# Second attention's output bank: three heads at rows 0, 34 and 68 in place of two at rows 0 and 64

## What is computed

```python
x = L0_attn_x                                   # (2, 512, 512)
x = _layernorm(x + _L0_attn_ref(x, ...))        # 32 heads of 128, sliding window
x = _layernorm(x + _L0_ffn_ref(x, ...))         # gated, 1376 wide
x = _layernorm(x + _L1_attn_ref(x, ...))        # 32 heads of 16, 8 key/value groups, causal
x = _layernorm(x + _L1_ffn_ref(x, ...))         # 512x512 and a low-rank part by 8 experts

# the attention of the second layer
scores = jnp.einsum('bhqd,bhkd->bhqk', q, k_h) / math.sqrt(HEAD_DIM)
scores = jnp.where(causal[None, None], jnp.finfo(scores.dtype).min, scores)
attn = jax.nn.softmax(scores, axis=-1)
ctx = jnp.einsum('bhqk,bhkd->bhqd', attn, v_h)
```

## Time and profile before

| | |
|---|---|
| median of 3 runs | 1215.43 us |
| profiled execution | 1214.89 us |
| its span, first to last instruction | 1213.3 us |
| granted TensorE clock, mean | 0.997 |
| TensorE matmul busy | 1180.8 us (97%), 6698 instructions |
| TensorE weight load busy | 1023.2 us (84%) |
| VectorE busy | 799.6 us (66%) |
| ScalarE busy | 752.5 us (62%) |
| GpSimd busy | 548.3 us (45%) |

### The profile page before, as it was taken

The page is one execution under the profiler, slowest core; times in us unless marked ns, Lnnn a source line. Parts: engine busy times, 40 slices in busy tenths (PEclk is TensorE's granted clock), DMA queues, the critical chain, the costliest instruction groups (busy, mean ns, idle before and its releaser), DMA issues. The chain is left out here.

```text
span 1213.3 us, 21135 instructions
## 1 busy us (share of the span) xinstructions
PE 1180.8 (97%) x6698; PEld 1023.2 (84%) x6698; DVE 799.6 (66%) x2575; ACT 752.5 (62%) x1758; POOL 548.3 (45%) x519
## 2 busy tenths in 40 slices
PE   7899999999999999999999999999999999999997
PEld 6788888888888888888888788888887999999886
DVE  6757776667766677766777722223458888888685
ACT  6656765566655567655665454441129999999624
POOL 4554454444533554534533233331136766676400
PEclk9999999999999999999999999999999999999999
DMA  6011110011110111101000022220002213220001
GB/s 223 18 44 36 35 36 28 22 43 27 46 34 12 44 36 35 36 27 35 27 1 27 18 70 78 61 97 1 18 20 53 65 41 108 48 48 21 1 1 70
DMA packets 30368, 51.28 MB, mean 42 GB/s; under 512 B 5680, under 2 KB 6576, under 8 KB 30256
## 3 DMA queue, kind: packets, MB, share of 16 engines
q1 hardware_dynamic: 29680, 48.85, 13.7%
q10 hardware_dynamic: 576, 1.05, 0.2%
HBM read 38.35 MB, written 2.10 MB: 33 GB/s over the span
## 5 line engine op out<-in xcount | busy, mean ns | idle before, releaser
L487 POOL TENSOR_TENSOR turned<-turned,sin 128x512 f32<-128x512 f32 x73 | 94.4, 1293 | 311.5 <-ACT turned L347 311.5
L363 ACT ACTIVATE probs<-probs,neg_max 128x256 f32<-128x256 f32 (+1 forms) x256 | 119.8, 473 | 14.0 <-DVE neg_max L580 14.0
L1484 ACT ACTIVATE a_probs<-a_probs,a_neg_max 128x512 f32<-128x512 f32 (+3 forms) x256 | 123.2, 571 | 0.1
L1720 DVE CUSTOM_DVE_ANT_0 a_probs<-bank,a_mask 128x512 f32<-128x512 f32 (+3 forms) x256 | 109.7, 485 | 0.2 <-PE bank L1949 0.2
L490 POOL TENSOR_TENSOR turned<-turned,by_cos 128x512 f32<-128x512 f32 x73 | 101.1, 1385 | 5.7
L96 PE MATMUL bank<-wo_hi,oT_hi 128*128 128x512 f32 x256 | 100.3, 392 | 1.7 <-DVE oT_lo L643 1.7
L734 PE MATMUL bank<-xT_hi,wq_hi 128*128 128x512 f32 x256 | 101.7, 397 | 0.0
L734 PE MATMUL bank<-xT_lo,wq_hi 128*128 128x512 f32 x256 | 100.2, 391 | 0.0
L734 PE MATMUL bank<-xT_hi,wq_lo 128*128 128x512 f32 x256 | 100.1, 391 | 0.0
L96 PE MATMUL bank<-wo_hi,oT_lo 128*128 128x512 f32 x256 | 99.9, 390 | 0.0
L96 PE MATMUL bank<-wo_lo,oT_hi 128*128 128x512 f32 x256 | 99.7, 389 | 0.0
(11 more groups left out here) (239 smaller groups left out, 3454.0 us busy)
## 6 DMA issues: line engine op xcount, KB each, us to landing
staged<-weights SPq DMA_DIRECT2D x70, 256.0 KB, 2.7
f_staged<-weights_f SPq DMA_DIRECT2D x33, 256.0 KB, 2.7
a_q_stack<-a_qT_hi SPq DMA_DIRECT2D x64, 64.0 KB, 2.0
rows<-x_rows SPq DMA_DIRECT2D x2, 1024.0 KB, 7.4
a_k_stack<-a_kT_hi SPq DMA_DIRECT2D x64, 32.0 KB, 2.0
a_q_stack<-a_qT_lo SPq DMA_DIRECT2D x32, 64.0 KB, 2.0
out<-rows SPq DMA_DIRECT2D x8, 256.0 KB, 2.0
a_raw<-weights_qkv SPq DMA_DIRECT2D x4, 384.0 KB, 4.9
```

Source lines behind the costliest of these rows:

```text
L363: act.activation(probs[:, s % 2, h, 0:width], probs[:, s % 2, h, 0:width], ACT.Exp, bias=neg_max[:, s % 2, h:h + 1], scale=SCALE0, accum_o ...
L487: pool.tensor_tensor(at, at, sin[:, :], ALU.mult).then_inc(sin_done, 1)
L1484: act.activation(row_probs(s, qt), row_probs(s, qt), ACT.Exp, bias=neg_max[:, h, qt:qt + 1], scale=-1.0).then_inc(exp_done, 1)
L1720: dve.tensor_tensor_reduce(row_probs(s, qt), ps_s[bank][:, at:at + seen], mask[:, SEQ - seen:SEQ], -SCALE1, HIGHEST, ALU.add, ALU.min, neg ...
```

## The change

The heads are grouped in packs of three (`PACK`), each head on 34 rows (`PACK_COLS`), at rows 0, 34 and 68, so that 102 rows (`OUT_ROWS`) are in use. A batch has 32 heads, so each batch begins with a pack of two and goes on with ten of three: 22 packs. A pack may run across two units. `PACK_OF` gives a head's pack and its place, `PACK_AT` the slot in which a pack is copied, turned, joined and finished: two slots after its last head's own slot, as before. The copy of the bank moves from ScalarE to VectorE, where it stands ahead of the maxima of its slot. `v_now` is 170 columns wide in place of 192, and the window is 102 columns in place of 128. The transposes move 102 columns and not 128.

```diff
+PACK_COLS = 2 * HD1 + 2
+PACK = 3
+OUT_ROWS = PACK * PACK_COLS
+V_AT = OUT_ROWS - PACK_COLS
+PACKS = []
+for _first in range(0, SLOTS1, SLOTS1 // BATCH):
+    _at, _end = _first, _first + SLOTS1 // BATCH
+    while _at < _end:
+        _size = PACK if (_end - _at) % PACK == 0 else 2
+        PACKS.append((_at, _size))
+        _at += _size
+PACK_OF = {_at + _n: (_i, _n) for _i, (_at, _size) in enumerate(PACKS) for _n in range(_size)}
+PACK_AT = {_at + _size + 1: _i for _i, (_at, _size) in enumerate(PACKS)}
...
-            def evacuate(n):
-                act.wait_ge(applied, 2 * (n + 1))
-                if n >= 1:
-                    act.wait_ge(o_turned, n)
-                act.activation(oT_now[:, :], ps_o[:, :], ACT.Copy).then_inc(o_read, 1)
...
-                if s % 2 == 1 and s >= 3:
-                    evacuate((s - 3) // 2)
...
-                if s % 2 == 1 and s >= 3:
-                    finish((s - 3) // 2)
+                if s in PACK_AT:
+                    finish(PACK_AT[s])
...
+            def evacuate(n):
+                dve.wait_ge(applied, PACKS[n][0] + PACKS[n][1])
+                if n >= 1:
+                    dve.wait_ge(o_turned, n)
+                dve.tensor_copy(oT_now[0:OUT_ROWS, :], ps_o[0:OUT_ROWS, :]).then_inc(o_read, 1)
+
             def join(n):
-                turned = ps_turn[:, :].rearrange("p (t h d) -> p t h d", t=SEQ_TILES, h=2)
+                size = PACKS[n][1]
+                turned = ps_turn[:, :].rearrange("p (t c) -> p t c", t=SEQ_TILES)[:, :, 0:size * PACK_COLS].rearrange(
+                    "p t (h d) -> p t h d", d=PACK_COLS)
...
             for s in range(SLOTS1 + 2):
+                if s in PACK_AT:
+                    evacuate(PACK_AT[s])
                 if s + AHEAD_MAXIMA < SLOTS1:
                     maxima(s + AHEAD_MAXIMA)
...
-                if s % 2 == 1 and 3 <= s < SLOTS1 + 1:
-                    join((s - 3) // 2)
+                if s in PACK_AT and s < SLOTS1 + 1:
+                    join(PACK_AT[s])
...
-                if h % 2 == 0 and s >= 2:
-                    pe.wait_ge(o_read, s // 2)
+                pack, place = PACK_OF[s]
+                if place == 0 and pack >= 1:
+                    pe.wait_ge(o_read, pack)
...
-                window = HALF - (h % 2) * HALF
+                window = V_AT - place * PACK_COLS
...
-                        mm = pe.matmul(ps_o[:, kb * P:SEQ], v_now[:, u % 2, kb, window:window + P],
+                        mm = pe.matmul(ps_o[0:OUT_ROWS, kb * P:SEQ], v_now[:, u % 2, kb, window:window + OUT_ROWS],
...
-                    mm = pe.transpose(ps_turn[:, j * P:(j + 1) * P], oT_now[:, j * P:(j + 1) * P], ident[:, :])
+                    mm = pe.transpose(ps_turn[:, j * P:j * P + OUT_ROWS], oT_now[0:OUT_ROWS, j * P:(j + 1) * P],
+                                      ident[0:OUT_ROWS, 0:OUT_ROWS])
...
-                if s % 2 == 1 and s >= 3:
-                    turn_output((s - 3) // 2)
+                if s in PACK_AT:
+                    turn_output(PACK_AT[s])
```

More of the change, by code:

```diff
@@ L1294, in attention1 @@
         oT_now = sb("oT_now", [P, SEQ])
-        o_sum = sb("o_sum", [P, SEQ_TILES, 2, HD1])
+        o_sum = sb("o_sum", [P, SEQ_TILES, PACK, HD1])
         by_at = aligned(nc.sbuf_base)
@@ L1298, in attention1 @@
         neg_max = sb("neg_max", [P, GROUP1, SEQ_TILES])
-        inv_sum = sb("inv_sum", [P, SEQ_TILES, 2])
+        inv_sum = sb("inv_sum", [P, SEQ_TILES, PACK])
         outT_hi, outT_lo = qT_hi, qT_lo
@@ L1614, in _ @@
             pool.wait_ge(pads_set, 2)
-            pool.memset(v_now[:, :, :, HALF + ONE_AT:HALF + ONE_AT + 1].bitcast(F32), 1.0).then_inc(pads_set, 1)
+            pool.memset(v_now[:, :, :, V_AT + ONE_AT:V_AT + ONE_AT + 1].bitcast(F32), 1.0).then_inc(pads_set, 1)
             def turn_rows(tile):
@@ L1636, in finish @@
             def finish(n):
-                u, pair = divmod(n, 2)
-                b, g = divmod(u, KV1)
-                at = g * GROUP_COLS + pair * PAIR_ROWS
+                first, size = PACKS[n]
+                b, head = divmod(first, HEADS1)
                 pool.wait_ge(summed, n + 1)
[L1641 to L1644, removed]
+                pool.tensor_tensor(o_tok[:, b * SEQ_TILES:(b + 1) * SEQ_TILES, head * HD1:(head + size) * HD1].rearrange(
+                    "p t (h d) -> p t h d", d=HD1), o_sum[:, :, 0:size, :],
+                                   inv_sum[:, :, 0:size].rearrange("p t (h a) -> p t h a", a=1).broadcast_to(
+                                       [P, SEQ_TILES, size, HD1]), ALU.mult).then_inc(finished, 1)
             def raise_diagonal(k):
@@ L1735, in join @@
                     dve.wait_ge(finished, n)
-                dve.reciprocal(inv_sum[:, :, :], turned[:, :, :, ONE_AT]).then_inc(inv_done, 1)
-                dve.tensor_copy(o_sum[:, :, :, :], turned[:, :, :, HD1:2 * HD1]).then_inc(low_read, 1)
+                dve.reciprocal(inv_sum[:, :, 0:size], turned[:, :, :, ONE_AT]).then_inc(inv_done, 1)
+                dve.tensor_copy(o_sum[:, :, 0:size, :], turned[:, :, :, HD1:2 * HD1]).then_inc(low_read, 1)
                 dve.wait_ge(low_read, n + 1)
                 dve.wait_ge(inv_done, n + 1)
-                dve.tensor_tensor(o_sum[:, :, :, :], turned[:, :, :, 0:HD1], o_sum[:, :, :, :], ALU.add).then_inc(summed, 1)
+                dve.tensor_tensor(o_sum[:, :, 0:size, :], turned[:, :, :, 0:HD1], o_sum[:, :, 0:size, :],
+                                  ALU.add).then_inc(summed, 1)
             for tile in range(TILES - 1):
@@ L1834, in _ @@
             low_out(0)
-            join(PAIRS1 - 1)
+            join(len(PACKS) - 1)
             for tile in range(1, 4):
@@ L1967, in apply @@
                     for part in (pT_hi, pT_lo):
-                        mm = pe.matmul(ps_o[:, kb * P:SEQ], v_now[:, u % 2, kb, window:window + P],
+                        mm = pe.matmul(ps_o[0:OUT_ROWS, kb * P:SEQ], v_now[:, u % 2, kb, window:window + OUT_ROWS],
                                        part[:, s % 2, piece, at:at + width],
-                                       start=(h % 2 == 0 and kb == 0 and part is pT_hi),
-                                       stop=(h % 2 == 1 and kb == KEY_TILES[-1] and part is pT_lo),
+                                       start=(place == 0 and kb == 0 and part is pT_hi),
+                                       stop=(place == PACKS[pack][1] - 1 and kb == KEY_TILES[-1] and part is pT_lo),
                                        skip_group_check=True)
@@ L2073, in _ @@
             turn_out(1)
-            turn_output(PAIRS1 - 1)
+            turn_output(len(PACKS) - 1)
             turn_out(2)
```

10 lines of the change are left out of this document (4 added, 6 removed).

## The result

| | before | changed |
|---|---|---|
| median | 1215.38 us (1215.1 to 1216.92, 4 runs) | 1201.42 us (1200.92 to 1203.3, 4 runs) |
| profiled execution, span | 1214.89, 1213.3 | 1201.25, 1199.6 |
| granted TensorE clock, mean | 0.997 | 0.996 |

What follows compares the result with a forecast made beforehand. ScalarE bound the second attention's loop, through its output copy L1501; TensorE would be next. 48 x (3.344 - 3.16) = 8.8, plus 0.4 and 0.5, less 1.2, gains 8.5 us: 1206.9, range 1202.9 to 1213.0.

Steps and rivals of the forecast that it cites:

- TensorE's terms: Second attention's loop: a slot costs TensorE 3.00 us, one with a turned output 3.48, so 9.48 for three slots.
- The copy's price: The copy of the bank from PSUM on VectorE, 102x512, estimated at 0.64 us, bounds 0.5 and 0.7.
- VectorE's pace: Rival, chance 0.20: VectorE with the added copy bounds the loop at 3.25 us a slot, gain 4.5, time 1211.
- The slow weight loads: Rival, chance 0.02: apply's loads of 102 columns go at half the pace, 0.22 us each, 11 us more, 1226.
- the 29.9 us: VectorE's wait for ScalarE ahead of L1728, read as idle time over the stage that makes the added copy fit.
- the hand-over loss: Ordinary slots: three engines within 4% of each other hand over less than ideally; 0.025 us x 48 = 1.2 taken off.
- the price of narrower operands: Apply's stationary and the transposes at 102 columns: taken as zero, bounds 0.06 us an apply either way, 0.1 a pack less.
- the gain of the last eight heavy slots: Slots 10 to 13 and 44 to 47, with weight halves on GpSimd: 0.4 us, only from calmer neighbours.
- my 3.22: Slots with a weight half: GpSimd bounds them at 3.02 us plus a share of finish, no difference by the change.
- The end of the loop: Last copy of the bank: 0.60 us on ScalarE becomes 0.64 on VectorE, which has nothing else ready; taken as zero.
- more than 12.5 us of gain: Rival, chance 0.03: narrower loads and transposes both shorten, ScalarE's 3.06 us a slot bounds, gain 14, at best 1201.
- The range's low end: Whole kernel, 1202.9 us: handing over free and both widths paying in part.

## Why the prediction was right in kind and too small

The gain by stretch, from the starts of TensorE's weight loads (turn of slot 0, then applies), with the forecast split in the same way:

| stretch | before | changed | gain | forecast | gain with 124 columns |
|---|---|---|---|---|---|
| turn 0 to apply 5 | 25.08 | 24.10 | 0.98 | 0.5 | 1.00 |
| 5 to 10 | 16.32 | 15.54 | 0.78 | 0.8 | 0.44 |
| 10 to 14 | 13.75 | 12.60 | 1.15 | 0.2 | 1.17 |
| 14 to 44 | 100.32 | 93.07 | 7.25 | 4.8 | 5.47 |
| 44 to 48 | 14.10 | 13.41 | 0.69 | 0.2 | 0.82 |
| 48 to 61 | 43.42 | 39.67 | 3.75 | 2.1 | 3.14 |
| 61 to 63 | 4.94 | 5.68 | -0.74 | 0 | -0.74 |
| sum | | | 13.9 | 8.5 | 11.3 |

The column with 124 columns is the run with copy and transposes of 124 rows too.

**What held.** Taking L1501 off ScalarE frees the loop, and TensorE becomes the bound: the pairs with VectorE's copy and the runs with wider operands show it. TensorE's terms held too, 3.00 a slot and 0.48 a turned output: the pairs take 6.46 for 6.48, the stage with 124 columns 94.85 for 95.3. The copy's price was 0.68 for 0.64. It lands beside the split and ahead of TensorE, with 0.46 of room where 0.35 was worked out. VectorE's pace was the nearest rival, and one more copy a pack made it true. The slow weight loads did not come: a load takes 168 ns, less than the 189 of before. One reading was off without harm: the 29.9 us that VectorE waited for ScalarE are those of the whole loop, not of the thirty slots, where that wait is 12.8 us.

In short, the step that failed is the sum. It named the right bound, but three of its terms were mis-sized: the hand-over loss (1.2 taken off, none there), the price of narrower operands (0 taken, 2.6 measured) and the gain of the last eight heavy slots (0.4 taken, 1.84 measured).

The difference, 5.4 us, is 2.6 from the widths (13.9 against 11.3 in the table) and 2.8 that were there with 124 columns too: 1.4 in the ordinary slots (9.05 against 7.7), 1.6 in the eight heavy ones (1.99 against 0.4), 0.5 in the first, less 0.74 at the end. By the same rates the four columns from 124 to 128 are some 0.5 more of the widths (an estimate, 2.5 x 4 / 22), within the 2.8.

**The hand-over term failed, 1.2 us.** I took 0.025 a slot off because a pair of before takes 6.69 where ScalarE's own work is 6.63. That loss belonged to ScalarE as the bound: it stands in one order behind results of the others. TensorE as the bound loses nothing that shows: with all its operands at 128 columns a pair takes 6.46 us, and the bare sum is 3.00 + 3.48. A loss at hand-overs isn't carried from one bounding engine to another without a row for it. Two smaller terms were missing from the ordinary slots and nearly cancel: they hold 17 turned outputs (2, 11 and 4 in the three stretches) and not 16, 0.5 us more, and slot 61, the last step of the stretch from apply 48, has no scores to make, so that its turn and the next stand 2.34 apart and not 2.96 (1108.58 and 1110.92), 0.6 us less. The missing scores are most of why the stretch behind slot 48 gained 1.0 more than forecast with 124 columns too; in the kernel before the same thirteen slots took 43.42, their full 13 x 3.344.

**The two widths failed, 2.6 us.** Stationary and transposes were taken as zero, with bounds of 0.06 an apply and 0.1 a pack. Measured are 0.04 an apply and 0.04 a pack for 22 columns. These were inside the bounds but only on one side: nothing in the trace spoke for a narrower operand that takes longer, while the earlier trace rows show ten loads one behind another at 0.11 us each, which shorter loads could only improve. Zero was the end of a one-sided range, not its middle.

**The heavy slots failed, 1.6 us.** I held that GpSimd is the bound there, at 3.02 + 0.2, and gave the last eight 0.4 us. In part it is: in the kernel before its casts of slots 45 to 48 follow one another without a gap, 3.43, 3.36 and 3.43 apart, from those of the earlier trace rows on:

```profile
1077.54 0.60 POOL L1631 CAST a_xT<-a_pT_raw 128x512 fp32r<-128x512 f32 x1
...
1080.97 0.61 POOL L1631 CAST a_xT<-a_pT_raw 128x512 fp32r<-128x512 f32 x1
```

But these are above my 3.22, the windows show 13.75 and 14.10 for four slots, and the first of these casts waited 0.74 for an apply. In the pairs with VectorE's copy GpSimd does the same work, and the eight slots take 12.93 and 13.33: the copy's place gives 0.8 us in each window. So these slots were held up by ScalarE's chain too, and the change reached them. The packs add 0.33 in slots 10 to 13 and nothing in 44 to 47 (13.41). The eight slots gained 1.84 us. That a late split held up ScalarE's copy, and with it the exponentials, is shown by the copy on ScalarE alone (4.42 us); in the kernel before only 0.2 us of such a wait is printed in each window. GpSimd's timeline of the changed kernel in slots 45 to 48:

```profile
1060.49 0.62 POOL L1636 CAST a_xT<-a_pT_raw 128x512 fp32r<-128x512 f32 x1
...
1063.58 0.61 POOL L1636 CAST a_xT<-a_pT_raw 128x512 fp32r<-128x512 f32 x1
...
1066.92 0.60 POOL L1636 CAST a_xT<-a_pT_raw 128x512 fp32r<-128x512 f32 x1
...
1070.47 0.61 POOL L1636 CAST a_xT<-a_pT_raw 128x512 fp32r<-128x512 f32 x1
```

3.09, 3.34 and 3.55 from cast to cast, without gaps: GpSimd is still the bound there, where a half meets a value split or a `finish`. A half without either goes through at the pace. This fits that spreading the work pays 1.9 us in this kernel; why it pays only 0.7 in the one before was not tested.

**Not in the sum.** Slots 0 to 4 gave 0.5 more than forecast; the cause is open. The end of the loop lost 0.74, and I had looked there only at the copy. GpSimd's timeline of the changed kernel ahead of the last apply:

```profile
1113.86 1.28 POOL L1638 TENSOR_TENSOR a_xT<-a_pT_raw,a_xT 128x512 fp32r<-128x512 f32 x1
1115.40 0.51 POOL L1645 TENSOR_TENSOR a_q_tok<-a_o_sum,a_inv_sum 128x192 f32<-128x192 f32 x1 [0.27 <-DVE a_o_sum L1752]
1115.86 0.61 POOL L1636 CAST a_xT<-a_pT_raw 128x512 fp32r<-128x512 f32 x1
```

With packs of three a `finish` falls between the last two splits: it waits 0.27 for the join and takes 0.51, and the last split and apply stand behind it. In the kernel before, these two splits followed each other directly:

```profile
1128.30 1.27 POOL L1633 TENSOR_TENSOR a_xT<-a_pT_raw,a_xT 128x512 fp32r<-128x512 f32 x1
1129.52 0.61 POOL L1631 CAST a_xT<-a_pT_raw 128x512 fp32r<-128x512 f32 x1
```

From split to cast it is 2.00 (1113.86 to 1115.86) in place of 1.22. The reading fits the 0.74; it has no experiment of its own.

**The chances.** I gave 0.03 to more than 12.5 us of gain, although that case needed nothing but each open width to pay and the hand-over to be free. I had set the two widths at zero and the hand-over as a loss, and no row spoke against any of the three. That case also took ScalarE as its bound; the changed kernel is still TensorE's, and ScalarE is busy without a gap only in the run with both spread work and narrow tiles, at 9.28 for three slots where 9.17 was worked out. The range's low end took the two widths in part; with its own bounds in full it would have been 1206.9 - 1.2 - 3 - 2 = 1200.7, and would have held 1201.4.

**Which loads are exposed.** 22 columns of stationary are worth 0.04 an apply and not 8 x 0.018 = 0.15, the eight loads' own difference. The 0.06 that I gave for an apply with loads of 85 in place of 107 ns isn't their sum either (8 x 22 ns is 0.18). The groups by shape say where it lies: from 102 to 124 columns the mean duration of apply's matmuls goes from 237 to 247 ns with 128 moving columns and from 297 to 306 with 256, two of each in an apply, 0.038 in all; those with 384 and 512 change by 1 to 3 ns. These ends are modelled, so this is a reading and no measurement of its own: the shorter loads show only beside the short matmuls.

## What to carry to other kernels

A copy in the written order of the bounding engine can cost more than its duration when it waits for a late partner: what stands behind it waits too (0.52 us in one slot here). Give it to an engine with slack, at the head of that engine's slot; behind other work the same copy cost 1.2 to 1.3 us a pack. Count how often the changed step really falls in a stage, and what its last slots leave out. When the bound moves to another engine, price the work left on that engine anew, its operand widths included, and don't bring along losses that belonged to the old bound. Look into what the engine that issues the loads waits for before moving the work that it waits for.

## What was not expected of the hardware

The duration of a weight load of float32r data falls with its columns: 189 ns at 128, 167 to 168 at 102, 139 at 68, 110 at 34, which is 0.84 ns a column on top of 82 ns. The Trainium skill, "TensorE: Matmul & The Clock Gate", section LDWEIGHTS, has a load at its columns over 1.2, thus 0.83 ns a column; the trace agrees in the slope. The section on Fast Weight Load of the same page would take the fast load away under 128 columns; the runs show no step between 128 and 102.

The four f32 transposes start (0.51 - 0.251) / 3 = 0.086 us apart with 102 moving columns and (0.60 - 0.272) / 3 = 0.109 with 128, although their weight loads keep 128 columns, so it isn't the loads' columns that set the spacing. The moving columns do, or the rows of the loads, which changed with them.

VectorE's copy from PSUM of 512 columns takes 682 ns with 102 rows and with 124, and 681 with 128 in pairs: between 102 and 128 rows it didn't depend on them. Reading the three heads of the join backwards cost nothing either (358 and 294 ns for its two large instructions, as forwards 358 and 295).
